# Batch 0's normalisation: GpSimd scales tiles 2 and 5, VectorE scales tile 7 alone and copies tile 7 out of PSUM in place of ScalarE

## What is computed

```python
x = x + attention(layernorm(x))   # conv 3x1024x768 -> q, k, v; 16 heads in blocks of 128 rows, causal; projection
x = x + ffn(layernorm(x))         # dense 1024x1024 with a gated low-rank part, 4 of 16 experts
# layernorm(x) = (x - mean) / sqrt(var + 1e-5), mean and var over the last axis
```

## Time and profile before

| | |
|---|---|
| median of 3 runs | 859.67 us (856.78 to 860.36) |
| profiled execution, its own time | 859.16 us |
| its span, first to last instruction | 857.2 us |
| mean granted TensorE clock | 0.978 |
| busy in the span | PE 803.8 us, DVE 460.2, ACT 394.0, POOL 198.4 |
| VectorE's first work on `ua` starts | 25.05 us |
| TensorE's first matmul on `ua` starts | 27.09 us |

### The profile page before, as it was taken

The page is one execution under the profiler, slowest core; times in us unless marked ns, Lnnn a source line. Parts: engine busy times, 40 slices in busy tenths (PEclk is TensorE's granted clock), DMA queues, the critical chain, the costliest instruction groups (busy, mean ns, idle before and its releaser), DMA issues.

```text
span 857.2 us, 14350 instructions
## 1 busy us (share of the span) xinstructions
PE 803.8 (94%) x5280; PEld 714.8 (83%) x5280; DVE 460.2 (54%) x1353; ACT 394.0 (46%) x1068; POOL 198.4 (23%) x178
## 2 busy tenths in 40 slices
PE   3899989999996699999999999999988999999997
PEld 3798877777784598888888888888878999999997
DVE  6879986778874234333333334333474445444442
ACT  5182443344233658777777777776771111111110
POOL 2110013222230224333333333433330001001000
PEclk9999999999998789999999999999999999999999
DMA  8646732533326230121253331203032223223111
GB/s 335 229 135 185 215 117 104 212 123 123 128 96 240 86 111 1 38 99 38 99 208 125 91 103 38 99 2 148 8 113 103 74 74 99 62 87 99 50 50 49
DMA packets 41353, 94.29 MB, mean 110 GB/s; under 512 B 9283, under 2 KB 18371, under 8 KB 39876
## 3 DMA queue, kind: packets, MB, share of 16 engines
q1 hardware_dynamic: 38980, 84.99, 29.3%
q0 software_dynamic: 2304, 8.39, 2.4%
HBM read 66.76 MB, written 26.21 MB: 108 GB/s over the span
## 4 chain that ended last, share of the span: by engine, by line
PE 72%; DVE 14%; ACT 5%; issue 3%; DMA 3%; POOL 2%; SPq 0%; DVEq 0%; ACTq 0%
PE net_psum L63 14%; PE net_psum L65 14%; PE net_psum L64 14%; PE net_psum L1088 8%; PE net_psum L1162 5%; PE net_psum L1173 4%; PE net_psum L1181 4%; POOL raw L442 2%; DVE raw L791 2%; PE net_psum L1073 2%; DVE raw L792 2%; PE net_psum L1216 2%; PE net_psum L1217 2%; PE net_psum L1218 2%; PE net_psum L1230 2%
## 5 line engine op out<-in xcount | busy, mean ns | idle before, releaser
L63 PE MATMUL net_psum<-fw_hi,xT_hi 128*128 128x354 f32 (+1 forms) x384 | 125.6, 327 | 0.7 <-DVE xT_lo L919 0.7
L65 PE MATMUL net_psum<-fw_hi,xT_lo 128*128 128x354 f32 (+1 forms) x384 | 124.4, 324 | 0.0
L64 PE MATMUL net_psum<-fw_lo,xT_hi 128*128 128x354 f32 (+1 forms) x384 | 124.4, 324 | 0.0
L459 POOL TENSOR_TENSOR pr<-pr,rrec 128x512 f32<-128x512 f32 x64 | 66.7, 1042 | 239.8 <-DVE rrec L854 239.8
L592 ACT ACTIVATE pr<-pr,negmax 128x128 f32<-128x128 f32 x256 | 99.1, 391 | 12.9 <-DVE negmax L861 12.9
L1088 PE MATMUL net_psum<-ua,wa 128*128 128x256 f32 x384 | 85.5, 385 | 3.3 <-DVE ua L749 3.3
L63 PE MATMUL net_psum<-c_hi,wqk_hi 128*128 128x256 f32 x256 | 78.6, 307 | 10.1 <-DVE c_lo L1030 7.2
L861 DVE CUSTOM_DVE_ANT_0 pr<-net_psum,mask 128x128 f32<-128x128 f32 x256 | 58.9, 288 | 53.7 <-PE net_psum L1162 53.6
L1088 PEld LDWEIGHTS net_psum<-ua,wa 128*128 128x128 f32 x384 | 73.7, 193 | 13.6 <-issue 3.5
L63 PE MATMUL net_psum<-x_hi,w_hi 128*128 128x512 f32 x192 | 77.5, 404 | 6.6 <-DVE w_lo L798 6.6
L65 PE MATMUL net_psum<-x_hi,w_lo 128*128 128x512 f32 x192 | 76.4, 398 | 0.0
(11 more groups left out here) (167 smaller groups left out, 1805.7 us busy)
## 6 DMA issues: line engine op xcount, KB each, us to landing
wa<-in_conv_w SPq DMA_DIRECT2D x24, 512.0 KB, 3.8
raw<-in_conv_w SPq DMA_DIRECT2D x24, 384.0 KB, 3.4
xn<-in_x SPq DMA_DIRECT2D x16, 512.0 KB, 10.4
xr<-in_x SPq DMA_DIRECT2D x8, 1024.0 KB, 4.9
x_scratch<-xr SPq DMA_DIRECT2D x8, 1024.0 KB, 4.1
x1t<-x_scratch SPq DMA_DIRECT2D x16, 512.0 KB, 4.1
out<-y POOLq DMA_DIRECT2D x16, 512.0 KB, 5.0
c_raw<-c_scratch SPq DMA_DIRECT2D x7, 768.0 KB, 4.8
```

What stands on the lines that cost most here:

```text
L63: pe.matmul(out, w_hi, x_hi, start=first, stop=False)
L64: pe.matmul(out, w_hi, x_lo, start=False, stop=False)
L65: return pe.matmul(out, w_lo, x_hi, start=False, stop=last)
L459: pool.tensor_tensor(pr[:, jj % 4], pr[:, jj % 4], rrec[:, jj % 4].unsqueeze(2).to_broadcast([P, UN, P]), ALU.mult).then_inc(s["p_ready"], 1)
```

## The change

GpSimd gets the scaling of tiles 2 and 5 (`tensor_scalar`, subtract the mean and multiply by `crstd`). It stands in GpSimd's program behind the power of the tile after (`power(0, 3)` and `power(0, 6)`). VectorE's `finish` for these two tiles keeps its wait and does nothing else; VectorE still scales tile 7. The last copy out of PSUM (tile 7) leaves ScalarE's program and stands in VectorE's ahead of `first_inputs`. TensorE waits for a new semaphore `xn_pool` beside `xn_dve`. ScalarE's scalings, which tile is turned when, all transfers and batch 1's counts stay.

```diff
--- before.py
+++ after.py
@@ -94,7 +94,8 @@
     NA = N * DUOS * NP4
     NK = MC * NP4
     AW, RR, WR, ST = 4, 3, 2, 4
-    DVE_SCALES = (2, 5, LT - 1)
+    POOL_SCALES = (2, 5)
+    DVE_SCALES = (LT - 1,)
     ROW = 4 * (QUADS + 1) - 1
     P0, P1, P2, P3 = 0, QUADS + 1, 2 * (QUADS + 1), 3 * (QUADS + 1)
     O0, O1, O2, O3 = 0, 1, 2, 3
@@ -105,7 +106,8 @@
 
     def act_scaled(n, j):
 
-        return LT + j + 1 - len(DVE_SCALES) if n else sum(i not in DVE_SCALES for i in range(j + 1))
+        other = DVE_SCALES + POOL_SCALES
+        return LT + j + 1 - len(other) if n else sum(i not in other for i in range(j + 1))
 
 
     NG = TOK // GT
@@ -237,7 +239,7 @@
         wa_loaded = [sp.sem(f"wa_loaded{i}") for i in range(AW)]
         raw_loaded = [sp.sem(f"raw_loaded{i}") for i in range(RR)]
         a_stored = [sp.sem(f"a_stored{i}") for i in range(ST)]
-        names = ("power_ready", "pads_ready", "stats_done", "mv_done", "var_ready", "rstd_ready", "shift_ready", "xn_act", "xn_dve",
+        names = ("power_ready", "pads_ready", "stats_done", "mv_done", "var_ready", "rstd_ready", "shift_ready", "xn_act", "xn_dve", "xn_pool",
                  "transposed", "xT_ready", "ua_part", "ua_ready", "a_done", "a_evac", "pair_ready", "u_ready", "x_hi_ready", "x_lo_ready",
                  "pre_ready", "ef_ready", "mix_ready", "w_hi_ready", "w_lo_ready", "unit_done", "ma_loaded", "t_ready", "halved", "add_step",
                  "add_done", "head_ready", "cy_ready", "c_stored", "bias_loaded", "qk_w_loaded", "early_loaded", "c5_hi_ready", "c5_lo_ready",
@@ -265,6 +267,10 @@
         def duo_acc(d, mi):
 
             return psum[:, 4 + 2 * (d % 2) + mi]
+
+        def tile_planes(n, j):
+
+            return stepped(xT, n * ROW + 32 * j, (N * ROW, DC), (QUADS + 1, 4), (1, 32))
 
         def pair(c, n, first, second):
 
@@ -474,6 +480,9 @@
             for n in range(N):
                 for j in range(LT):
                     power(n, j)
+                    if n == 0 and j - 1 in POOL_SCALES:
+                        pool.wait_ge(s["rstd_ready"], j)
+                        pool.tensor_scalar(xn[:, n, j - 1], xn[:, n, j - 1], cmv[:, n, j - 1, 0:1], crstd[:, n, j - 1:j], ALU.subtract, ALU.mult).then_inc(s["xn_pool"], 1)
             for k in range(NK):
                 mix(k)
             pool.wait_ge(s["unit_done"], NP4 * LAST + 1)
@@ -505,8 +514,7 @@
 
             def tile_out(n, j):
                 act.wait_ge(s["transposed"], LT * n + j + 1)
-                planes = stepped(xT, n * ROW + 32 * j, (N * ROW, DC), (QUADS + 1, 4), (1, 32))
-                act.activation(planes, turned(n, j).rearrange("p b (c t k) -> p (b c) k t", k=4, t=32), ACT.Copy).then_inc(s["xT_ready"], 1)
+                act.activation(tile_planes(n, j), turned(n, j).rearrange("p b (c t k) -> p (b c) k t", k=4, t=32), ACT.Copy).then_inc(s["xT_ready"], 1)
 
             def first_out(d):
                 act.wait_ge(s["a_done"], NP4 * (d + 1))
@@ -665,11 +673,10 @@
                     act.activation(b_hi[:], b_raw[:], ACT.Copy).then_inc(s["b_split_hi"], 1)
 
             for j in range(LT):
-                if j not in DVE_SCALES:
+                if j not in DVE_SCALES + POOL_SCALES:
                     scale(0, j)
                 if j:
                     tile_out(0, j - 1)
-            tile_out(0, LT - 1)
             first_out(0)
             for j in range(3):
                 scale(1, j)
@@ -734,6 +741,8 @@
 
             def finish(n, j):
                 dve.wait_ge(s["rstd_ready"], LT * n + j + 1)
+                if n == 0 and j in POOL_SCALES:
+                    return
                 if n == 0 and j in DVE_SCALES:
                     dve.tensor_scalar(xn[:, n, j], xn[:, n, j], cmv[:, n, j, 0:1], crstd[:, n, j:j + 1], ALU.subtract, ALU.mult).then_inc(s["xn_dve"], 1)
                 else:
@@ -997,6 +1006,8 @@
                 if j:
                     finish(0, j - 1)
             finish(0, LT - 1)
+            dve.wait_ge(s["transposed"], LT)
+            dve.tensor_copy(tile_planes(0, LT - 1), turned(0, LT - 1).rearrange("p b (c t k) -> p (b c) k t", k=4, t=32)).then_inc(s["xT_ready"], 1)
             dve.wait_ge(s["pads_ready"], 1)
             dve.wait_ge(s["xT_ready"], LT)
             for c in range(0, DC, 2):
@@ -1063,7 +1074,8 @@
         def _(pe):
             def normalised(n, j):
                 if n == 0:
-                    wait(pe, s["xn_dve"], j + 1 - act_scaled(0, j))
+                    wait(pe, s["xn_dve"], sum(i in DVE_SCALES for i in range(j + 1)))
+                    wait(pe, s["xn_pool"], sum(i in POOL_SCALES for i in range(j + 1)))
                 pe.wait_ge(s["xn_act"], act_scaled(n, j))
 
             def transpose_tile(n, j):
```

## The result

| | median us (lowest to highest, runs) | ratio to before, 95% interval |
|---|---|---|
| before | 859.22 (856.74 to 860.50, 20) | |
| changed | 862.44 (857.51 to 864.80, 20) | 1.0035 [1.0024, 1.0047] |

The change costs 0.35%: 3.0 us by the ratio, 3.2 us by the medians. That is inside the 0.5% called "same", but 0.7 us above the range, and 2.6 us above the forecast of 859.8. The profiled execution of the changed kernel took 858.45 us with a span of 856.6. It is one of the shorter of the 20, and its span alone would say "0.6 us faster than before". What the change does has to be read from the front of the trace, where both profiles are alike up to 12 us but for a shift of 0.21 us (first transpose at 10.57, before 10.36).

The account below looks back on a forecast made before the run. TensorE, busy 94%, was taken to be bound by when `ua` starts: 0 for tiles 2 and 5, 0 to 0.05 for scaling 6, 0.05 to 0.1 for the copy moved it from 25.05 to 25.15, giving 859.8 us (range 857.0 to 861.7).

Parts of the forecast that it names:

- GpSimd's scaling, price: GpSimd's scaling of one 128x1024 tile: 1.6 us, with bounds of 0.8 and 2.4 us.
- Tile 2: GpSimd scales it 13.0 to 14.6, TensorE turns it by 15.6, before ScalarE asks at 16.13; cost 0.
- The held shift: VectorE's shifts of tiles 3 and 6 wait until GpSimd's scalings end; without this the sum is 0.15 us better.
- The formula: Start of `ua` from GpSimd's two scaling times D2 and D5; 25.1 for 1.6 each, each microsecond above costing one.
- Rival 1: GpSimd's scaling is as slow as its two-input sum, 2.4 us twice: `ua` 1.6 late, 861.4 us; chance 0.08.
- The copy: VectorE's copy of tile 7 takes 1.2 us instead of ScalarE's 1.04; net plus 0.05 to 0.1 us.
- The place: Front of the kernel: everything turns on when `ua` starts, 25.05 before; powers of tiles 3 and 6 back at 0.55.
- One for one: Each microsecond by which `ua` starts earlier or later reaches the kernel's end in full.
- Rival 2: TensorE's low clock after idling before `ua` falls later or lasts 3 us longer: 1.5 us, 861.3; chance 0.04.
- Rival 3: GpSimd's first scaling carries a one-time cost: at 7.6 us `ua` starts at 31.1, time 865.8; chance 0.03.

Follow-up runs that it names:

- warm_after: Changed kernel with extra identity transposes on TensorE ahead of tile 2's, tile 5's and the first matmul on `ua`; 860.18 us, ratio 1.0020 to before.
- pool_quarter: Changed kernel with GpSimd's two scalings covering only the first 256 of 1024 columns, the rest left unscaled; 859.31 us, ratio 0.9995 to before.
- Pool_forms: Changed kernel with GpSimd only multiplying by `crstd`: one-operation tensor_scalar on tile 2, tensor_tensor with repeated column on tile 5; 860.98 us (1 run).
- pool_tile2: Changed kernel with only tile 2's scaling on GpSimd, tile 5's back on VectorE; 861.26 us, ratio 1.0033 to before.
- late_3: Kernel before with tile 7's copy moved to VectorE and done four times instead of once; 863.61 us, ratio 1.0051 to before.
- late_6: Kernel before with tile 7's copy moved to VectorE and done seven times instead of once; 867.28 us, ratio 1.0099 to before.
- pool_tile5: Changed kernel with only tile 5's scaling on GpSimd, tile 2's back on VectorE; 861.04 us, ratio 1.0033 to before.
- pool_only: Changed kernel with the copy of tile 7 back on ScalarE, both scalings still on GpSimd; 862.31 us, ratio 1.0026 to before.
- warm_tile5: Kernel with only tile 5's scaling on GpSimd, plus extra identity transposes ahead of tile 5's and the first matmul on `ua`; 861.53 us, ratio 1.0034.
- powers_first: Changed kernel with each GpSimd scaling moved one power later, behind the powers of tiles 4 and 7; 864.09 us, ratio 1.0059 to before.

## Why the prediction was wrong

**The step that failed: "GpSimd's scaling, price".** I took 1.6 us and called 2.4 the upper bound, because GpSimd's sum of two 128x1024 tensors takes 2.40 "and the scaling reads one". It measured 3.79. The bound assumed that the tensors read set the price. The runs show that the form of the instruction does: one tensor in takes 1.04, 2.85 or 3.79 us, and one more operation 0.94. The nearest row on GpSimd that I had was of another instruction, and a row of another instruction bounds nothing from above. The Trainium skill, "GPSIMD Engine Reference", section 3.1, gives the 1.8 cycles an element, an estimate of 1.54 us, that I weighed beside the rows; this case measured two and a half times that.

**Tile 2 "hidden, with 0.5 us to spare; at 2.4 us it would be 0.3 late".** The account was right: ScalarE asks for the tile at 16.13. With 3.79 TensorE begins at 17.03 and the slack is gone. But I priced its transposes at 0.9 us, and those of tiles 2 and 3 took 3.68 us, not 1.94. That is a second term, on ScalarE's string; warm_after takes it away, but `ua` gains only 0.3 us by it, since GpSimd's string is as long. This term was mis-sized even for a short scaling: in pool_quarter tile 2 took 1.97 us behind a wait of 0.22. With 1.6 us and a start at 14.7 it would have been turned at about 16.7, an estimate, 0.5 us after ScalarE asks for it, and not 0.5 before.

**The held shift.** It didn't happen. The shift of tile 3 ran at 14.15 in the middle of GpSimd's scaling and took 0.23 us instead of 0.15; that of tile 6 at 20.93, the same. The earlier trace rows showed VectorE held beside a tensor_tensor on GpSimd, and I carried this to tensor_scalar. Pool_forms has both in one profile, VectorE's rows:

```profile
13.98 0.15 DVE L752 SCALAR_TENSOR_TENSOR cshift<-cmv,crstd 128x1 f32<-128x1 f32 x1
...
19.82 0.91 DVE L752 SCALAR_TENSOR_TENSOR cshift<-cmv,crstd 128x1 f32<-128x1 f32 x1
```

Beside GpSimd's tensor_scalar with one operation (13.01 to 15.86) the shift takes 0.15; beside its tensor_tensor (18.82 to 20.71) the same instruction lasts until 20.73. By the Trainium skill, "SBUF — State Buffer", section "SBUF: two separate sides", of a VectorE operation with two SBUF inputs and a GpSimd operation that reads SBUF the one that starts first keeps the shared ports and the other waits. That holds here beside the tensor_tensor (0.91 us) and not beside the tensor_scalar (0.15 to 0.23 us). At 1.6 us this step would have cost 0.15 us and no more; it made the formula too pessimistic, not the forecast too low.

**The formula** `ua` = 21.9 + D2 + D5 gives 29.5 for twice 3.79; measured 28.32, or 28.1 without the front's 0.21. It had the second scaling start at 17.1 + D2 = 20.9; it started at 19.96, because the shift wasn't held. It followed only GpSimd's string, and the TensorE and ScalarE one beside it is as long (pool_tile2: `ua` at 27.83 with scaling 2 alone).

**Rival 1** was this mechanism with too small a price: 861.4 for 2.4 us. With 3.79 the same formula gives 859.16 + 29.5 - 25.05 = 863.6, 1.2 above the median, and less the 0.9 us by which scaling 5 started earlier (19.96, not 20.9) 862.7. The rival got 0.08, since the bound kept everything above 2.4 out.

**What held.** The copy: 1.2 forecast, 1.23 measured, and no effect on the end that the times show (0.9991). The place: the loss is made before `ua` starts, and the powers of tiles 3 and 6 back at 0.55 us. "One for one": 3.1 us later (3.27 less 0.21), 3.0 to 3.2 us longer, and in the profiles of late_3 and late_6 the delay reaches the end whole. That the medians agree to 0.1 us is luck, though. `ua` of one profile doesn't foretell a version's median so closely: pool_tile5 lost 2.8 us with `ua` 4.1 later, pool_only 2.2 with 4.5, warm_tile5 2.9 with 1.8, each with an interval of about 1.1 to 1.5 us to either side. **Rival 2**, the clock: the low stretch moved after all, since TensorE's waits changed; in the changed kernel it shows in one profile and not in the other, and makes 2.8 us between them. How much of the 3.2 us between the medians it makes is open; that it doesn't make the loss by itself is seen in pool_quarter, whose profile has the low stretch too (80 matmuls in 20.48) and whose median has no loss. **Rival 3**, a one-time cost: excluded, the first scaling took 3.79 and the second 3.78.

**Still open.** Why the fillers' gain in the front (up to 2.3 us in warm_tile5) is not in the medians. One profile each can't tell, since the time behind the first piece also differs between profiles (span less the piece's end: 752.1 us in before, 749.9 after, 755.0 in warm_after), by more than the gain in question.

## What to carry to other kernels

A price on an engine is bounded only by a row of the same instruction there: on GpSimd one 128x1024 tensor in and out took from 1.04 to 3.79 us by the instruction alone. Before work is moved to a slow engine, find who asks for its result in program order and how soon (here 3 us after the input was ready), and count as well what the waiting engine does afterwards at a lower clock. When undoing a part of a change brings little back, look for a second string that ends together with the one undone; the chain that ended last names only one.

## What the runs showed of the hardware

- GpSimd, 128x1024 float32: tensor_scalar 3.79 us with two operations on columns, 3.65 on constants, 2.85 with one operation, tensor_tensor with a repeated column 1.89, copy 1.04; the first grows by 3.33 ns with each element of a row.
- VectorE's own tensor_scalar beside GpSimd's is slowed, not held: in powers_first 1.69 us instead of 0.81, done at 23.11 while GpSimd ran to 25.17:

```profile
21.42 1.69 DVE L747 TENSOR_SCALAR xn<-xn,cmv,crstd 128x1024 f32<-128x1024 f32 x1 [0.60 <-POOL crstd L442]
```

- TensorE in a wait: in pool_tile5, twice, the granted clock fell to 0.50 within a wait of 3.3 us. After the 2.78 us wait for tile 2 16 transposes took 3.68 us, and the record says 1.00 at 17 to 18 us; with work in the wait 16 took 1.97. In pool_only the same 16 took 3.52 us behind the same wait, and there the record says 0.66, 0.50, 0.50 and 0.64 from 17 to 21 us. So a granted clock of 1.00 in the record didn't mean the full rate of transposes here. Whether the rate fell in the wait or had not yet risen isn't settled: the 16 transposes of tiles 0 and 1, the first work of all, took 3.67 us too.
- In late_6, with the longest wait (10.97 us before the first matmul on `ua`), the granted clock was 0.50 in every stretch from 29 to 39 us; the 80 matmuls still took 19.31, no more than with a wait of 3.41. In the same profile it had been 0.50 at 19 to 22 us behind waits of 0.86 and 0.94 us: the 16 transposes of tiles 4 and 5 took 3.50 us, where late_3, the same up to there, had 1.94.
